# Interleaving three small layers with the gate products of the next column block, in a four-layer graph network on one core

## The chip, the core and the metric

The kernel runs on one core of a Trainium2 chip. The metric is the device time of one execution in microseconds (us). The core has a matrix engine (TensorE, "PE" in the profile; its weight loads are "PEld"), a vector engine (VectorE, "DVE"), an activation engine (ScalarE, "ACT"), GpSimd ("POOL") and the engine that issues transfers here (SyncE, "SP"). Each engine runs its own instructions strictly in the order of the program, and they wait for one another through semaphores. TensorE writes its results to eight banks of PSUM, `PS[0]` to `PS[7]`; ScalarE and VectorE carry them from there to SBUF.

## The reference

Four graph layers work one after the other on 1875 nodes with 256 features. The change lies in the second one, after its messages have been summed into `agg` per node. What follows there is, for each node on its own:

```python
gates = agg @ W_ih.T + b_ih + b_hh
i, f, g, o = jnp.split(gates, 4, axis=-1)
c = jax.nn.sigmoid(i) * jnp.tanh(g)
hn = jax.nn.sigmoid(o) * jnp.tanh(c)
x = jax.nn.relu(hn @ W1.T + b1)
x = jax.nn.relu(x @ W2.T + b2)
return x @ W3.T + b3
...
x = _layernorm(x + _L1_gnn_ref(...), axis=-1)
```

The gate `f` isn't used, so 3 x 256 gate features are computed: six pieces of 128. `W1` takes 256 features to 128, `W2` 128 to 128, `W3` 128 to 256.

## The kernel before

All engines' programs are written out by hand, with waits by hand; nothing plans or reorders them. The 1875 nodes are padded to 1920, which are `NC` = 5 column blocks of `CN` = 384 nodes. In the gate stage a block c goes through these steps:

- TensorE, `gates(c)`: six products (j = 0 to 5), each of two parts k, into `PS[0]` to `PS[5]` (L1796). A product j of block c waits until ScalarE has emptied the same bank of block c-1 (`gate_ev`). In the trace a float32 product of 384 columns shows as two matmul records, so one block's gates are 24 records.
- ScalarE, L748: six evacuations with Sigmoid or Tanh into the tile `GT`, j = 0 to 5. The first of block c waits for `hn_ready` of block c-1, since there is only one `GT`.
- VectorE, L1332: `CC` = the product of gates 0, 1 with 2, 3; it waits for evacuation 3 of the block. ScalarE, L750: tanh of `CC`. VectorE, L1337: `HN` = `CC` times gates 4, 5; this counts `hn_ready`.
- The three small layers: TensorE multiplies by W1 into `PS[6]` (L1813, waits for `hn_ready`), ScalarE applies Relu into `X1` (L757); TensorE multiplies by W2 into `PS[7]` (L1816), ScalarE applies Relu into `X2` (L759); TensorE adds the bias row and multiplies by W3 for three tiles of 128 nodes, into `PS[6]` and `PS[7]` (L1820, L1821). This is called x1, x2, x3 below.
- VectorE, L1349 and L1350: adds the result to `X` and counts `x3_add`; x1 of the next block waits for that. Only then does VectorE come to L1332 of the next block.

TensorE's order is: gates(0); 15 small products that count degrees (L1804); and then for each block c: gates(c+1), x1(c), x2(c), x3(c). ScalarE's order is, per block: six evacuations, tanh, X1, X2. In blocks 2 and 3 ScalarE also converts a piece of the adjacency counts between tanh and X1 (`early_cast`, L733, in a branch). In block 1 VectorE also splits four bias rows (L1221 to L1227) behind `HN`. In the last block VectorE normalises the first twelve node tiles between `HN` and the adds, with a square root from ScalarE (`ln_sqrt(5, ...)`, L671).

When x3 of the last block is done (`x3_mm`), SyncE loads six weights of the third layer (L477) over the place of the old ones, and TensorE's products of the third layer (`project`, L1831 and L1833) wait for them.

Of the kernel before, what the change touches and what calls it, by code (L numbers as in the profile page):

```python
# [29 lines left out]
ACT = mybir.ActivationFunctionType  # L30
# [6 lines left out]
NT = -(-N // P)  # L37
# [72 lines left out]
CN = 3 * P  # L110
NC = NP // CN
# [57 lines left out]
def build(nc, rec, x, xT, edge0, w0, a0l, a0r, cols, hrow, wrel, brow, wih, w1, w2, w3, b3, wp1, bp1, wl1, bl1, wr1, wp2, bp2, wl2, bl2, wr2,  # L169
          wt3, a3l, a3r, out):  # L170
    ctx = ExitStack()
    with ctx:
# [26 lines left out]
        BC = sb("bias_cols", [P, 32], F32)  # L199
# [13 lines left out]
        PS = [BANKS[:, 512 * i:512 * (i + 1)] for i in range(8)]  # L213

        def ar(off, *dims, dt=None):
            n = 1
            for d in dims:
                n *= d
            v = AR[:, off:off + n]
            if len(dims) == 2:  # L220
                v = v.rearrange("p (a b) -> p a b", b=dims[1])
            elif len(dims) == 3:
                v = v.rearrange("p (a b c) -> p a b c", b=dims[1], c=dims[2])
            return v
# [123 lines left out]
        GT = ar(A_B1, 6, CN)  # L348
        CC, HN, X1, X2 = ar(A_B1 + 6 * CN, 2, CN), ar(A_B1 + 8 * CN, 2, CN), ar(A_B1 + 10 * CN, CN), ar(A_B1 + 11 * CN, CN)
# [11 lines left out]
        s = {n: sem(n) for n in names}  # L361
# [210 lines left out]
        def _(act):  # L572
            a = nc.scalar
# [95 lines left out]
            def ln_sqrt(n, t0, t1):  # L669
                act.wait_ge(s["var_ready"], n)  # L670
                a.activation(RS[:, t0:t1], MV[:, t0:t1, 1], ACT.Sqrt).then_inc(s["std_ready"], 1)  # L671
# [64 lines left out]
            def early_cast(v, c):  # L736
                with act.If(large < 1):
                    cast2(v, c, False)
                with act.If(large >= 1):
                    cast2(v, c, True)  # L740

            funcs = (ACT.Sigmoid, ACT.Sigmoid, ACT.Tanh, ACT.Tanh, ACT.Sigmoid, ACT.Sigmoid)
            for c in range(NC):
                for j in range(6):
                    act.wait_ge(s["gate_mm"], 6 * c + j + 1)
                    if j == 0 and c:
                        act.wait_ge(s["hn_ready"], c)
                    a.activation(GT[:, j, :], PS[j][:, 0:CN], funcs[j], bias=BC[:, 20 + j:21 + j]).then_inc(s["gate_ev"], 1)  # L748
                act.wait_ge(s["c_ready"], c + 1)
                a.activation(CC, CC, ACT.Tanh).then_inc(s["tc_ready"], 1)  # L750
                if c in (2, 3):
                    act.wait_ge(s["bias_ready"], 2)
                    early_cast(0, c - 2)
                if c == NC - 1:
                    ln_sqrt(5, 0, NT - 3)
                act.wait_ge(s["x1_mm"], c + 1)
                a.activation(X1, PS[6][:, 0:CN], ACT.Relu, bias=BC[:, 18:19]).then_inc(s["x1_ev"], 1)  # L757
                act.wait_ge(s["x2_mm"], c + 1)
                a.activation(X2, PS[7][:, 0:CN], ACT.Relu, bias=BC[:, 19:20]).then_inc(s["x2_ev"], 1)  # L759
            ln_sqrt(6, NT - 3, NT)  # L760
            for q in range(4):
                xt_evac(1, q)
# [704 lines left out]
        def _(pe):  # L1467
# [95 lines left out]
            for i in range(4 * NT):  # L1563
                if i in between:
                    between[i]()
                t, c = i // 4, i % 4
# [147 lines left out]
            def transpose_x(n, q, src, ready, before):  # L1714
                pe.wait_ge(ready, before + q + 1)
                if n >= 2 and q >= 2:
                    xt_ready(n, q - 2)
                for k in range(2):
                    for j in range(min(4, NT - 4 * q)):
                        ins = tr(PS[xt_bank(n, q) + k][:, P * j:P * (j + 1)], src[:, 4 * q + j, P * k:P * (k + 1)], ident[:, :])  # L1720
                    ins.then_inc(s["xt_mm"], 1)
# [65 lines left out]
            pe.wait_ge(s["agg_evd"], 1)  # L1787
            pe.wait_ge(s["agg_eva"], 4)

            def gates(c):  # L1790

                for j in range(6):
                    if c:
                        pe.wait_ge(s["gate_ev"], 6 * c - 5 + j)
                    for k in range(2):
                        ins = mm(PS[j][:, 0:CN], WIH[:, k, P * j:P * (j + 1)], XT[:, k, CN * c:CN * (c + 1)],  # L1796
                                 start=(k == 0), stop=(k == 1))
                    ins.then_inc(s["gate_mm"], 1)

            gates(0)  # L1800
            pe.wait_ge(s["cnt_red"], 1)
            for t in range(NT):
                w = min(P, NW - P * t)
                ins = mm(PS[7][0:w, t:t + 1], CNTS[:, P * t:P * t + w], ones[:, 0:1], start=True, stop=True)  # L1804
            ins.then_inc(s["cnt_mm"], 1)
            for c in range(NC):
                if c + 1 < NC:
                    gates(c + 1)
                pe.wait_ge(s["hn_ready"], c + 1)
                if c:  # L1810
                    pe.wait_ge(s["x3_add"], c)
                for k in range(2):
                    ins = mm(PS[6][:, 0:CN], W1s[:, k, :], HN[:, k, :], start=(k == 0), stop=(k == 1))  # L1813
                ins.then_inc(s["x1_mm"], 1)
                pe.wait_ge(s["x1_ev"], c + 1)
                mm(PS[7][:, 0:CN], W2s, X1, start=True, stop=True).then_inc(s["x2_mm"], 1)  # L1816
                pe.wait_ge(s["x2_ev"], c + 1)
                for j in range(3):
                    o = PS[6 + j // 2][:, D * (j % 2):D * (j % 2 + 1)]
                    mm(o, ones16[0:3, :], BP[0:3, 2, :], start=True, stop=False)  # L1820
                    ins = mm(o, X2[:, P * j:P * (j + 1)], W3s, start=False, stop=True)  # L1821
                ins.then_inc(s["x3_mm"], 1)
            for q in range(4):
                transpose_x(1, q, X, s["ln_done"], 4)

# [111 lines left out]
```

## Time and profile before

| | |
|---|---|
| median of 3 runs | 1783.98 us (1782.76 to 1784.89) |
| the profiled execution: its own time | 1781.72 us |
| span of the profiled execution, first to last instruction | 1780.0 us |
| busy in the span: PE, DVE, ACT, POOL | 80%, 65%, 42%, 31% |
| mean granted TensorE clock (share of full speed) | 0.76 |
| gate stage: first gate product to the last small layer's end | 1364.52 to 1448.05 us |

Busy shares are averages over stages with different limits. The stage of the change is about 84 us of the span, and the granted clock in it is at either of two levels, 1.00 (2.4 GHz) or 0.50 (1.2 GHz).

### The profile page before, as it was taken

The page shows a single profiled execution, that of the slowest core. Times are in us where ns is not written, and L with a number is a line of the kernel's source. Part 1 is how long each engine was busy: PE and PEld are TensorE (multiplying, and loading weights), DVE is VectorE, ACT ScalarE, POOL GpSimd, SP SyncE. Part 2 cuts the span into 40 slices and gives each one's busy share as a digit, 9 for nine tenths or more (in the row PEclk, how much of TensorE's full clock was granted, in tenths as well). Part 3 has the DMA queues.
Part 4 walks back from the last instruction along what each step waited for, and adds up shares of the span by engine and source line. Part 5 has one row for each costly group of instructions (what it writes and reads, how often), then busy time and mean ns, then how long its engine had stood idle before and what let it go on. Part 6 is the DMA issues. An engine that isn't in the chain of part 4 may idle for free.

```text
span 1780.0 us, 21845 instructions
## 1 busy us (share of the span) xinstructions
PE 1422.1 (80%) x5158; PEld 758.0 (43%) x5158; DVE 1154.4 (65%) x2990; ACT 749.8 (42%) x1243; POOL 546.0 (31%) x517
## 2 busy tenths in 40 slices
PE   5897987777777777773499999798999989989840
PEld 2454643411111111112277777454445447758630
DVE  6323543399999999999989988751180443543727
ACT  1333443477777777772000000236774435416022
POOL 0103777777777777771000000000000000000023
PEclk9997555755555555555599999898999979999965
DMA  4534666655555555552098888000000010000023
GB/s 163 167 133 154 210 210 213 211 185 187 185 186 185 179 187 184 186 185 85 25 322 275 266 273 256 1 1 26 1 1 2 0 36 0 2 12 1 1 62 74
DMA packets 84507, 223.90 MB, mean 126 GB/s; under 512 B 18456, under 2 KB 27588, under 8 KB 83908
## 3 DMA queue, kind: packets, MB, share of 16 engines
q1 hardware_dynamic: 60452, 158.01, 25.4%
q0 software_dynamic: 23968, 64.77, 14.0%
q8 instruction: 51, 0.84, 0.2%
q14 instruction: 36, 0.29, 0.1%
HBM read 140.09 MB, written 82.63 MB: 125 GB/s over the span
## 4 chain that ended last, share of the span: by engine, by line
PE 43%; DVE 20%; issue 14%; POOL 6%; DMA 2%; ACT 2%; DVEq 2%; SPq 0%; POOLq 0%
PE bank L1776 14%; PE bank L1711 13%; POOL arena L557 6%; DVE arena L1095 4%; DVE arena L1096 3%; DVE adjacency L1102 3%; PE bank L1796 2%; DVE arena L1137 2%; PE bank L1833 2%; PE bank L1758 2%; PE bank L1733 2%; DMA arena<-feat_table,arena 1%; PE bank L1865 1%; DVEq L372 1%; PE bank L1862 1%
## 5 line engine op out<-in xcount | busy, mean ns | idle before, releaser
L557 POOL DMA_INDIRECT arena<-feat_table,arena x469 | 508.8, 1085 | 240.1 <-issue 227.9
L1650 PE MATMUL bank<-arena 128*128 128x480 f16 x586 | 337.0, 576 | 122.0 <-DVE arena L1096 116.0
L639 ACT ACTIVATE arena<-bank 128x480 uint16<-128x480 f32 x586 | 333.4, 572 | 118.1 <-PE bank L1650 111.6
L565 POOL DMA_INDIRECT arena<-al_table,edge_ends x15 | 14.8, 985 | 917.4 <-DMA al_table<-arena 913.2
L1102 DVE TENSOR_TENSOR adjacency<-adjacency,arena 128x480 uint16 x586 | 235.5, 402 | 9.9 <-DVE arena L1115 6.2
L1650 PEld LDWEIGHTS bank<-arena 128*128 128x128 f16 x586 | 61.0, 104 | 398.3 <-DVE arena L1096 312.0
L1711 PE MATMUL bank<-arena 128*128 x966 | 229.6, 392 | 0.9 <-issue 0.3
L1096 DVE TENSOR_SCALAR arena<-iota,arena 128x480 f16<-128x480 f16 x586 | 199.2, 340 | 0.0
L1711 PEld LDWEIGHTS bank<-arena 128*128 128x128 f32 x966 | 173.4, 190 | 57.3 <-issue 36.4
L1193 DVE TENSOR_TENSOR arena<-arena 128x1024 f32<-128x1024 f32 x118 | 140.1, 1214 | 16.4 <-DMA arena<-edge_rows 14.5
L1776 PE MATMUL bank<-arena 128*128 128x472 f16 x720 | 146.2, 367 | 3.9 <-ACT arena L713 3.9
L1095 DVE TENSOR_SCALAR arena<-iota,arena 128x128 f16<-128x128 f16 x586 | 145.9, 249 | 1.3 <-ACT adjacency L603 1.3
L713 ACT ACTIVATE arena<-adjacency 128x1888 f16<-128x1888 uint16 x30 | 109.0, 3638 | 34.9 <-PE bank L1776 34.9
L1570 PE MATMUL bank<-arena 128*128 128x512 f32 x240 | 108.8, 608 | 5.7 <-ACT arena L588 3.0
L1776 PE MATMUL bank<-count_chunks,message_halves 128*128 128x472 f32 x480 | 103.4, 377 | 2.1 <-DVE message_halves L1293 2.1
L1776 PEld LDWEIGHTS bank<-arena 128*128 128x128 bf16 x720 | 71.1, 99 | 79.3 <-ACT arena L713 4.7
L671 ACT ACT_TABLE_LOAD x2 | 2.6, 1283 | 240.0 <-DVE ln_mean_var L1239 240.0
L1776 PEld LDWEIGHTS bank<-count_chunks,message_halves 128*128 128x128 f32 x480 | 90.0, 188 | 15.5 <-issue 2.9
L1613 PE MATMUL bank<-arena 128*128 x588 | 75.7, 189 | 17.1 <-DVE arena L1052 11.3
L733 ACT ACTIVATE count_chunks<-adjacency 128x944 fp32r<-128x944 uint16 (+1 forms) x30 | 69.9, 2335 | 39.8 <-PE bank L1776 39.8
L1613 PEld LDWEIGHTS bank<-arena 128*128 128x128 f16 x588 | 60.1, 105 | 48.4 <-issue 35.0
L1200 DVE TENSOR_TENSOR arena<-iota,arena 128x1024 f32<-128x1024 f16 (+1 forms) x61 | 73.8, 1210 | 7.0 <-PE bank L1711 6.9
(294 smaller groups left out, 1598.0 us busy)
## 6 DMA issues: line engine op xcount, KB each, us to landing
arena<-edge_rows SPq DMA_DIRECT2D x117, 520.0 KB, 4.7
edge_rows<-arena SPq DMA_DIRECT2D x67, 520.0 KB, 2.9
edge_rows<-arena SPq DMA_DIRECT2D x67, 390.0 KB, 2.6
feat_table<-arena SPq DMA_DIRECT2D x60, 260.0 KB, 2.1
arena<-feat_table,arena POOLq DMA_INDIRECT x469
arena<-in_w SPq DMA_DIRECT2D x1, 2048.0 KB, 9.7
arena<-in_xT SPq DMA_DIRECT2D x1, 1920.0 KB, 18.0
arena<-in_x SPq DMA_DIRECT2D x1, 1792.0 KB
```

Source lines behind the costliest of these rows:

```text
L557: g.indirect_dma_start(out=PLACE[k][:, t - lo, :], out_offset=None, in_=feat_t, in_offset=bass.IndirectOffsetOnAxis(ap=IE[:, t:t + 1], axi ...
L639: a.activation(EV[st % AS].rearrange("p r k -> p (r k)"), PS[4 + st % 4][:, 0:R2 * KW], ACT.Copy)\
L713: a.activation(chunk(CH1, c % 2, wide), ADJ[:, r, :].rearrange("p (n s) -> p n s", s=SH)[:, :, sh], ACT.Copy).then_inc(s["chunk_ready"], 1)
L1095: v.tensor_scalar(OHS[st % AS], iota128[:, :], lo, None, ALU.is_equal)
L1096: v.tensor_scalar(OHK[st % AS], iota480[:, :], key, None, ALU.is_equal).then_inc(s["a_oh"], 1)
L1102: v.tensor_tensor(dst, dst, EV[st % AS], ALU.add).then_inc(s["a_add"], 1)
L1193: v.tensor_tensor(rows, rows, al, ALU.mult).then_inc(s["r_wgt"], 1)
L1570: ins = mm(PS[c][:, :], XT0[:, k, P * t:P * (t + 1)], W0[:, k, 512 * c:512 * (c + 1)], start=(k == 0), stop=(k == 1))
L1613: ins = mm(PS[4 + g % 2][:, 3 * H * k:3 * H * (k + 1)], KO[g % 3][:, lo:lo + P], ERW[:, bass.ds(offs[k], 3 * H)], start=True, stop=True)
L1650: mm(PS[4 + st % 4][:, 0:R2 * KW], OHS[st % AS], OHK[st % AS], start=True, stop=True).then_inc(s["a_mm"], 1)
L1711: mm(BANKS[:, bass.ds(out_at, D)], OHR[:, (st // RG) % ORING, P * (st % RG):P * (st % RG + 1)], FBf[:, bass.ds(places[st % RK] >> 12, D)], ...
L1776: ins = mm(PS[4 * fo + j][:, 0:CW], m[:, P * fo:P * (fo + 1)], ch[:, CW * j:CW * (j + 1)], start=(c == 0 and q == 0), stop=(c == n - 1 and ...
```

## The change

TensorE no longer computes all six gate products of block c+1 ahead of the small layers of block c. It computes three of them, then x1(c), the fourth, x2(c), the fifth, x3(c), the sixth. ScalarE's order follows, and two other pieces move on it: the conversions of blocks 2 and 3 come behind X2 in place of ahead of X1, and the square root of the last block is written ahead of the (there empty) gate evacuations. VectorE's and SyncE's programs are the same.

```diff
             funcs = (ACT.Sigmoid, ACT.Sigmoid, ACT.Tanh, ACT.Tanh, ACT.Sigmoid, ACT.Sigmoid)
+            def gate_out(c, j):
+
+                act.wait_ge(s["gate_mm"], 6 * c + j + 1)
+                if j == 0 and c:
+                    act.wait_ge(s["hn_ready"], c)
+                a.activation(GT[:, j, :], PS[j][:, 0:CN], funcs[j], bias=BC[:, 20 + j:21 + j]).then_inc(s["gate_ev"], 1)
+
+            for j in range(6):
+                gate_out(0, j)
             for c in range(NC):
-                for j in range(6):
-                    act.wait_ge(s["gate_mm"], 6 * c + j + 1)
-                    if j == 0 and c:
-                        act.wait_ge(s["hn_ready"], c)
-                    a.activation(GT[:, j, :], PS[j][:, 0:CN], funcs[j], bias=BC[:, 20 + j:21 + j]).then_inc(s["gate_ev"], 1)
                 act.wait_ge(s["c_ready"], c + 1)
                 a.activation(CC, CC, ACT.Tanh).then_inc(s["tc_ready"], 1)
+                if c == NC - 1:
+                    ln_sqrt(5, 0, NT - 3)
+                if c + 1 < NC:
+                    for j in range(3):
+                        gate_out(c + 1, j)
+                act.wait_ge(s["x1_mm"], c + 1)
+                a.activation(X1, PS[6][:, 0:CN], ACT.Relu, bias=BC[:, 18:19]).then_inc(s["x1_ev"], 1)
+                if c + 1 < NC:
+                    gate_out(c + 1, 3)
+                act.wait_ge(s["x2_mm"], c + 1)
+                a.activation(X2, PS[7][:, 0:CN], ACT.Relu, bias=BC[:, 19:20]).then_inc(s["x2_ev"], 1)
                 if c in (2, 3):
                     act.wait_ge(s["bias_ready"], 2)
                     early_cast(0, c - 2)
-                if c == NC - 1:
-                    ln_sqrt(5, 0, NT - 3)
-                act.wait_ge(s["x1_mm"], c + 1)
-                a.activation(X1, PS[6][:, 0:CN], ACT.Relu, bias=BC[:, 18:19]).then_inc(s["x1_ev"], 1)
-                act.wait_ge(s["x2_mm"], c + 1)
-                a.activation(X2, PS[7][:, 0:CN], ACT.Relu, bias=BC[:, 19:20]).then_inc(s["x2_ev"], 1)
+                if c + 1 < NC:
+                    for j in (4, 5):
+                        gate_out(c + 1, j)
...
-            def gates(c):
-
-                for j in range(6):
+            def gates(c, js):
+
+                for j in js:
+                    if c == NC:
+                        break
...
-            gates(0)
+            gates(0, range(6))
...
             for c in range(NC):
-                if c + 1 < NC:
-                    gates(c + 1)
+                gates(c + 1, range(3))
                 pe.wait_ge(s["hn_ready"], c + 1)
...
                 ins.then_inc(s["x1_mm"], 1)
+                gates(c + 1, (3,))
                 pe.wait_ge(s["x1_ev"], c + 1)
                 mm(PS[7][:, 0:CN], W2s, X1, start=True, stop=True).then_inc(s["x2_mm"], 1)
+                gates(c + 1, (4,))
                 pe.wait_ge(s["x2_ev"], c + 1)
...
                 ins.then_inc(s["x3_mm"], 1)
+                gates(c + 1, (5,))
```

On TensorE, from the degree counts on, block 0 stood like this before (one row may stand for several instructions, `x12` for the six gate products of two parts each; L1796 is a gate product, L1813 x1, L1816 x2, L1820 and L1821 x3):

```order
3655 L1804 MATMUL bank<-ones,arena 96x1
3656 L1796 MATMUL bank<-arena 128x384 x12
3657 L1813 MATMUL bank<-arena 128x384 x2
3658 L1816 MATMUL bank<-arena 128x384
3659 L1820 MATMUL bank<-arena,ones 128x256
3660 L1821 MATMUL bank<-arena 128x256
```

The same place in the changed program, where a gate product is L1810, x1 is L1826, x2 L1830, and x3 L1835 and L1836:

```order
3655 L1818 MATMUL bank<-ones,arena 96x1
3656 L1810 MATMUL bank<-arena 128x384 x6
3657 L1826 MATMUL bank<-arena 128x384 x2
3658 L1810 MATMUL bank<-arena 128x384 x2
3659 L1830 MATMUL bank<-arena 128x384
3660 L1810 MATMUL bank<-arena 128x384 x2
3661 L1835 MATMUL bank<-arena,ones 128x256
3662 L1836 MATMUL bank<-arena 128x256
3663 L1835 MATMUL bank<-arena,ones 128x256
3664 L1836 MATMUL bank<-arena 128x256
3665 L1835 MATMUL bank<-arena,ones 128x256
3666 L1836 MATMUL bank<-arena 128x256
```

So three gate products now stand ahead of x1, one between x1 and x2, and one between x2 and x3. At the end of the small layers of block 3 the changed TensorE program goes on like this:

```order
3698 L1835 MATMUL bank<-arena,ones 128x256
3699 L1836 MATMUL bank<-arena 128x256
3700 L1810 MATMUL bank<-arena 128x384 x2
3701 L1826 MATMUL bank<-arena 128x384 x2
3702 L1830 MATMUL bank<-arena 128x384
```

The sixth gate product of block 4 now stands between x3(3) and x1(4), where nothing stood. On ScalarE, before, the tanh of block 2 (L750), its conversion (L733, in the taken branch of two), its two Relus (L757, L759) and the gates of block 3 (L748) stood like this:

```order
492 L750 ACTIVATE arena<-arena 128x768
493 L737 COMPARE_AND_BRANCH
494 L733 ACTIVATE count_chunks<-adjacency 128x1888
495 L737 UNCONDITIONAL_BRANCH
496 L739 COMPARE_AND_BRANCH
497 L733 ACTIVATE arena<-adjacency 128x1888
498 L739 UNCONDITIONAL_BRANCH
499 L757 ACTIVATE arena<-bank,bias_cols 128x384
500 L759 ACTIVATE arena<-bank,bias_cols 128x384
501 L748 ACTIVATE arena<-bank,bias_cols 128x384 x6
```

The same block in the changed program, where tanh is L754 and the Relus are L761 and L765:

```order
496 L754 ACTIVATE arena<-arena 128x768
497 L748 ACTIVATE arena<-bank,bias_cols 128x384 x3
498 L761 ACTIVATE arena<-bank,bias_cols 128x384
499 L748 ACTIVATE arena<-bank,bias_cols 128x384
500 L765 ACTIVATE arena<-bank,bias_cols 128x384
501 L737 COMPARE_AND_BRANCH
502 L733 ACTIVATE count_chunks<-adjacency 128x1888
503 L737 UNCONDITIONAL_BRANCH
504 L739 COMPARE_AND_BRANCH
507 L748 ACTIVATE arena<-bank,bias_cols 128x384 x2
```

The conversion moved from ahead of both Relus to between the second Relu and the last two gate evacuations of block 3. No load of an activation table was added or moved among these rows.

## Rows read from the trace of the kernel before

**Rows 1.** Chain that ended last, blocks 0 and 1: start us, us, what.
```profile
1378.43 7.85 PE bank L1796 x24
1386.28 1.30 PE bank L1813 x4
...
1392.42 7.74 PE bank L1796 x24
1400.16 1.30 PE bank L1813 x4
...
1401.48 0.59 ACT arena L757
...
1402.12 0.93 PE bank L1816 x2
...
1403.07 0.59 ACT arena L759
...
1403.70 0.28 PE bank L1820
...
1406.29 7.74 PE bank L1796 x24
```

**Rows 2.** The same chain, from x1 of block 3 to the third layer.
```profile
1427.90 1.30 PE bank L1813 x4
...
1434.08 0.02 DVEq L1347
...
1437.95 2.60 PE bank L1813 x4
...
1448.05 0.41 SPq L477
...
1455.41 0.39 PE bank L1831
```

**Rows 3.** Timeline of DVE: start us, us, line, what, [idle before <-releaser].
```profile
1380.96 0.96 DVE L1337 TENSOR_TENSOR arena<-arena 128x768 f32<-128x768 f32 x1 [0.91 <-ACT arena L750]
...
1395.25 0.96 DVE L1337 TENSOR_TENSOR arena<-arena 128x768 f32<-128x768 f32 x1 [0.91 <-ACT arena L750]
...
1402.98 1.27 DVE L1227 SCALAR_TENSOR_TENSOR arena<-arena,ident 3x1024 bf16<-3x1024 bf16 x1
```

**Rows 4.** Timeline of ACT, block 2, and two conversions in a row later.
```profile
1408.32 0.84 ACT L750 ACTIVATE arena<-arena 128x768 f32<-128x768 f32 x1 [1.84 <-DVE arena L1332]
1409.07 3.63 ACT L733 ACTIVATE count_chunks<-adjacency 128x1888 fp32r<-128x1888 uint16 x1
1415.36 0.58 ACT L757 ACTIVATE arena<-bank,bias_cols 128x384 f32<-128x384 f32 x1 [2.65 <-PE bank L1813]
...
1532.24 7.14 ACT L733 ACTIVATE count_chunks<-adjacency 128x1888 fp32r<-128x1888 uint16 x2
```

**Rows 5.** Windows: busy by engine, then PEclk (granted clock), DMA share, GB/s.
```profile
1378.30:1434.00 55.70, 50.32 (x158) 27.01 (x157) 20.72 (x33) 26.22 (x38) 0.00 (x0) 1.00 0.00 0
1438.00:1448.00 10.00, 8.65 (x16) 3.62 (x17) 6.16 (x29) 1.58 (x4) 0.00 (x0) 0.52 0.00 0
1532.90:1533.80 0.90, 0.90 (x4) 0.67 (x4) 0.00 (x0) 0.90 (x1) 0.00 (x0) 1.00 0.00 0
1533.90:1537.30 3.40, 3.40 (x9) 2.59 (x9) 0.88 (x2) 3.40 (x2) 0.00 (x0) 0.50 0.00 0
1651.80:1653.20 1.40, 1.40 (x6) 0.90 (x7) 0.00 (x0) 0.00 (x0) 0.00 (x0) 1.00 0.06 12
1653.40:1656.80 3.40, 3.40 (x9) 2.05 (x7) 1.33 (x4) 0.00 (x0) 0.00 (x0) 0.50 0.00 0
```

**Rows 6.** Timeline of PE, the two places of rows 5 that follow an idle time.
```profile
1532.89 1.13 PE L1862 MATMUL bank<-arena 128*128 128x256 f32 x4 [2.48 <-DVE arena L1315]
...
1651.78 1.13 PE L1862 MATMUL bank<-arena 128*128 128x256 f32 x4 [2.48 <-DVE arena L1315]
```

## The prediction, made before the changed kernel ran

> **What bounds the kernel now.** I read the chain of work that ended last first, in order of time, because only what stands on it can shorten the run. From the end of the degree counts to the last gate product this chain is TensorE, broken by two short ScalarE pieces per block [rows 1]. One block is 13.87 us (1392.42 to 1406.29): 7.74 us of gate products, 1.30 us of x1, then a Relu of 0.59 us on ScalarE, x2, another Relu of 0.59 us, and x3 from 1403.70 to 1406.29, 2.59 us. During both Relus TensorE stands still: x1 starts at 1400.16 and is 1.30 long, but x2 starts only at 1402.12, 0.66 us after x1's end; x2 starts at 1402.12 and x3 at 1403.70, 1.58 us for two matmul records. At the steady rate of 7.74 / 24 = 0.3225 us per record, two take 0.65 us, so 0.93 us of that is waiting for the drain and the Relu.
>
> Then I followed the chain to where the stage hands over [rows 2]. x3(3) ends at 1434.08; x1(4) starts at 1437.95, 3.87 us later, because VectorE's adds, CC, tanh on ScalarE and HN stand between and no TensorE work is left. x1(4) to x3(4) then take 10.10 us (1437.95 to 1448.05). The same layers of block 3 take 6.18 us (1427.90 to 1434.08). The windows say why: the granted clock is 1.00 from 1378.3 to 1434.0 and 0.52 from 1438 to 1448 [rows 5], nearly all of it at the lower of the two levels. At 1448.05 SyncE starts the next layer's weights, and that layer's first product waits for them until 1455.41. What comes behind is tied to that moment, so whatever the stage saves, the span should save.
>
> **The change part by part.** No arithmetic is added or removed; the costs are all order.
>
> *Start.* Before, x1(0) comes behind all of gates(1), 7.85 us from 1378.43, and starts at 1386.28 [rows 1]. Now three of six products stand ahead of it: 7.85 / 2 = 3.92 us, so x1(0) could start at 1382.35. It needs HN(0), which ends at 1380.96 + 0.96 = 1381.92 [rows 3], 0.4 us earlier. Gain 3.9 us. The cover is thin: if HN(0) were later by more than 0.4 us, the rest would be lost one for one.
>
> *Steady blocks.* TensorE's own work per block is 7.74 + 1.30 + 0.65 + 2.59 = 12.28 us. The fourth gate product (two parts, 7.74 / 6 = 1.29 us) stands where TensorE waited 0.66 us for X1. With x1 starting at time 0, x1 ends at 1.30, the gate product at 2.59, and X1 is ready at 1402.12 - 1400.16 = 1.96: no wait. x2 runs from 2.59, the fifth gate product to 4.53; X2 is ready 1.58 us after x2's start, at 4.17: no wait. x3 ends at 7.12, the sixth product at 8.41, three products of the next block at 12.28. What could be late there is HN. Before, x1(4) came 3.87 us behind x3(3) through exactly this sequence [rows 2], so HN is ready at 7.12 + 3.87 = 10.99, 1.3 us before x1 wants it. A block is then 12.28 in place of 13.87: three periods between x1(0) and x1(3) give 3 x 1.59 = 4.8 us.
>
> *ScalarE's order in blocks 2 and 3.* The conversion (3.63 us) was covered by 2.65 us of idle time behind it [rows 4]. Now the last two gate evacuations queue behind it, and behind these tanh, HN and x1. X2 ends at about 4.1, the conversion at 7.8, the fifth evacuation (0.58) at 8.3; the sixth can't start before its product at 8.41, and ends at 9.0. Tanh is due when CC is there: it started 2.03 us after x3's end before (1408.32 against 1406.29 [rows 1, 4]), so at 9.15. The conversion fits with about nothing over. The two branches around it are the unknown: from below nothing, since two conversions in a row took 7.14 us, less than 2 x 3.63 [rows 4]; from above 2.65 us, the idle time that could hide them before. I take nothing, as the row of two conversions is the nearest. Block 2 has the 1.3 us of HN's slack as well.
>
> *VectorE in block 1.* The bias split begins behind HN and ended 8.04 us after it (1396.21 to 1404.25 [rows 3]). HN(1) now ends 1.3 us before x1(1), so the split ends at 6.7 after it, before x3(1) at 7.12. Nothing is lost.
>
> *End.* x1(4) needs HN(4). From x1(3) it comes at 10.99, where it was 10.05 (1427.90 to 1437.95): three gate products of 1.29 us now stand between the small layers, and only the Relu waits pay for two of them. Loss 0.9 us.
>
> *The clock.* TensorE's idle time ahead of x1(4) shrinks from 3.9 us to 10.99 - 8.41 = 2.6 us. Whether the clock falls again decides up to 10.10 - 6.18 = 3.9 us. The nearest rows are two idle times of 2.48 us later in the kernel [rows 6]. After both, dense products began at 1.00 and the clock then stood at 0.50: still full 0.9 us after the first restart and 1.4 us after the second, low from 1.0 and 1.6 us on [rows 5, 6]. So I expect the fall here too, but with some 0.9 us of x1(4) at full speed, work that takes twice as long at half: 1.30 against 2.60 us for x1 [rows 2]. I take 0.9 us of gain, with bounds of 0 and 3.9.
>
> The Trainium skill ("TensorE: Matmul & The Clock Gate", section "Why this matters for your kernels") advises to keep idle gaps between bursts of matmuls short, and the gap from which it warns of a slow restart is longer than the wait forecast here. By that page x1(4) to x3(4) would run at full speed and the gain would be 7.8 + 3.9 = 11.7 us. The two rows after 2.48 us of idle time speak against it, and the measurement decides.
>
> **Sum.** 3.9 + 4.8 - 0.9 = 7.8 us, and 0.9 for the clock: 8.7 us. The profiled execution took 1781.72 us, so its like would take 1773.0. The median of the runs shown is 2.3 us above that execution, so I forecast 1783.98 - 8.7 = 1775.3 us.
>
> **The rivals.** *The clock stays up.* Gain 11.7 us, 1772.3 us. For it: a shorter idle time than before, and 1.00 throughout the blocks with their waits. Against it: rows 5 and 6.
>
> *HN comes late in the blocks.* The branches hold ScalarE, or the evacuations pile up more than I have laid out. With 2.65 us in both blocks, block 2 loses 2.65 - 1.3 and block 3 all of it: 4.0 us, gain 4.7, 1779.3 us. For it: three pieces of work end within 0.2 us of each other in my layout. Against: the two conversions back to back.
>
> *The gain is taken back at the weights.* If the third layer waited for something other than the weights, say VectorE's normalisation, the stage would be shorter and the span not: 1784 us. Against it: the chain goes through the SyncE issue at 1448.05 and the landing before 1455.41, with no wait of another kind between.
>
> *Slower: the clock falls inside a block.* With products and waits interleaved otherwise, TensorE might drop to half speed among the gates. Rows 2 price it: x1 takes 2.60 for 1.30, so a block at half speed costs some 12 us more, and one such block outweighs the 8.7 us: 1783.98 - 8.7 + 12 = 1787.3 us. It decides from the first whole block. Against it: 1.00 from 1378.3 to 1434.0 with 0.66 and 0.93 us of waits per block, and the change shortens these.
>
> **How the numbers follow.** Chances: forecast 0.62, clock stays up 0.12, HN late 0.13, no gain 0.08, slower 0.05. The four times of before spread over 3.1 us (1781.72 to 1784.89), so each case carries some 1.5 us either way. The range from 1771.0 to 1779.5 holds the first two cases and about half of the third, some 8 in 10. A change under 0.2% (3.6 us) can't be told from none. Faster needs less than 1780.4 us: the first two cases and most of the third, 0.86. Same takes the fourth and the rest of the third, 0.09; slower 0.05.
>
> **What the changed profile would show.** Between the sixth evacuation of block 0 and x1(4), TensorE without idle time; x1 of successive blocks 12.3 us apart; x1(0) some 3.9 us behind the end of the counts; no wait of the gate products for evacuations. The idle time ahead of x1(4) would be 2.6 us, with granted clock falling within x1(4) or just behind it. I am wrong if x1 of some block waits for HN, if in blocks 2 and 3 ScalarE's fifth evacuation starts much later than the end of the conversion, or if x1(4) to x3(4) take about 6 us.

## The result, and the profile after

The changed kernel takes 1772.19 us (median of 4 runs, 1768.48 to 1773.56), the kernel before 1783.37 us in the runs beside it. The ratio is 0.9941, with a 95% interval of 0.9914 to 0.9967: faster by 0.6%, and the whole interval lies below 1. In two more sets of runs (e10 and e12 below) the same kernel stood at 0.9941 (0.9922 to 0.9960) and 0.9931 (0.9907 to 0.9956). The forecast was 1775.3 us.

The profiled execution took 1768.48 us, with a span of 1766.8 us. That is 13.2 us shorter than the profiled span before; 2.8 us of it lie ahead of the gate stage (first gate product at 1361.70 us, before at 1364.52), where nothing was changed. So stages are compared below from the first gate product on.

The chain that ended last, from the end of the degree counts to x1 of block 1, answers to [rows 1] (start us, us, what; gate products are now L1810, x1 L1826, x2 L1830, x3 L1835 and L1836):

```profile
1375.54 3.98 PE bank L1810 x12
1379.52 1.29 PE bank L1826 x4
1380.81 1.29 PE bank L1810 x4
1382.10 0.65 PE bank L1830 x2
1382.75 1.29 PE bank L1810 x4
1384.04 0.21 PE bank L1835
...
1386.56 5.16 PE bank L1810 x16
1391.72 1.29 PE bank L1826 x4
```

No ScalarE piece and no waiting is left in it: the chain is TensorE from end to end. x1(1) starts 12.20 us after x1(0); it was 13.87 us. x2 costs 0.65 us on the chain, where it cost 0.93. Between x1 and x2 and between x2 and x3 stands a gate product of 1.29 us, as laid out.

The end of the stage on the same chain answers to [rows 2] (L1344 is CC, L754 tanh, L1349 HN, L671 the square root, L761 the Relu X1, L477 the weights, L1847 the third layer's first product):

```profile
1423.14 1.12 PE bank L1810 x4
1424.26 0.88 DVE arena L1344
...
1425.17 0.85 ACT arena L754
...
1426.04 0.96 DVE arena L1349
1427.00 1.00 DVE ln_stats L1244 x3
...
1429.17 0.21 ACT ln_rstd L671
1429.38 0.48 ACT arena L761
...
1435.67 0.41 SPq L477
...
1443.43 0.28 PE bank L1847
```

One piece of it was in no part of the prediction: the chain doesn't go through x1(4), but through VectorE's statistics and the square root, behind which X1 stands on ScalarE. TensorE's timeline shows what that does (in brackets the idle time ahead and what ended it):

```profile
1427.05 1.56 PE L1826 MATMUL bank<-arena 128*128 128x384 f32 x4 [2.63 <-DVE arena L1349]
1429.90 0.91 PE L1830 MATMUL bank<-arena 128*128 128x384 f32 x2 [1.29 <-ACT arena L761]
1431.49 0.28 PE L1835 MATMUL bank<-arena,ones 3*128 3x256 bf16 x1 [0.67 <-ACT arena L765]
```

The idle time ahead of x1(4) is 2.63 us (forecast 2.6; before 3.9). Ahead of x2(4) it is 1.29 us in place of 0.67: with x1 at full speed, its Relu now has to wait for the square root. Before, x1(4) at half speed ended later than the root (root done at 1440.28 us, X1 from 1440.58), so the root held up nothing:

```profile
1437.95 2.59 PE L1813 MATMUL bank<-arena 128*128 128x384 f32 x4 [3.92 <-DVE arena L1337]
1441.22 1.65 PE L1816 MATMUL bank<-arena 128*128 128x384 f32 x2 [0.67 <-ACT arena L757]
```

ScalarE in block 2, where the conversion was moved, answers to [rows 4] (L748 gate evacuations, L765 the Relu X2, L733 the conversion):

```profile
1407.17 0.58 ACT L765 ACTIVATE arena<-bank,bias_cols 128x384 f32<-128x384 f32 x1
1407.65 3.61 ACT L733 ACTIVATE count_chunks<-adjacency 128x1888 fp32r<-128x1888 uint16 x1
1411.17 0.57 ACT L748 ACTIVATE arena<-bank,bias_cols 128x384 f32<-128x384 f32 x1
1412.27 0.58 ACT L748 ACTIVATE arena<-bank,bias_cols 128x384 f32<-128x384 f32 x1 [0.54 <-PE bank L1810]
1412.97 0.84 ACT L754 ACTIVATE arena<-arena 128x768 f32<-128x768 f32 x1
```

The branches cost nothing that shows: the fifth evacuation starts as the conversion ends, and ScalarE then waits 0.54 us for the sixth product. The layout had left 0.1 us there.

The granted clock by windows (busy by engine, then PEclk) answers to [rows 5]:

```profile
1375.40:1427.00 51.60, 49.03 (x158) 27.38 (x157) 23.56 (x38) 30.01 (x40) 0.00 (x0) 1.00 0.00 0
1427.05:1431.90 4.85, 2.88 (x8) 1.27 (x9) 4.47 (x24) 1.52 (x4) 0.00 (x0) 1.00 0.00 0
1432.00:1435.70 3.70, 3.70 (x10) 1.69 (x9) 1.66 (x7) 0.00 (x0) 0.00 (x0) 0.50 0.00 0
1443.40:1462.60 19.20, 19.14 (x75) 11.53 (x75) 5.95 (x14) 5.38 (x14) 0.00 (x0) 1.00 0.00 1
```

The clock still falls in the last small layers, but 4.9 us after x1(4)'s start and not within x1. The last row is new: the first products of the third layer run at full speed. Before, they did not:

```profile
1455.40:1462.20 6.80, 6.79 (x15) 3.82 (x15) 0.85 (x2) 0.77 (x2) 0.00 (x0) 0.50 0.01 2
```

All runs by stage, in us from their profiles: A from the first gate product to the start of x1(4); B from there to the start of the third layer's weights; C from that to the third layer's first product; D from that to the start of the product of its fifteenth and last node tile. "Idle" is TensorE's idle time ahead of x1(4). Each row is one profiled execution.

| run | A | idle | B | C | D | sum |
|---|---|---|---|---|---|---|
| before | 73.4 | 3.92 | 10.1 | 7.4 | 20.9 | 111.8 |
| before again (e8) | 73.4 | 3.92 | 10.2 | 7.6 | 20.7 | 111.9 |
| changed | 65.4 | 2.63 | 8.6 | 7.8 | 17.8 | 99.5 |
| changed again (e10) | 65.6 | 2.63 | 8.4 | 7.3 | 17.8 | 99.1 |
| changed, third (e12) | 65.6 | 2.62 | 8.4 | 7.5 | 17.8 | 99.3 |
| e1, TensorE's order only | 64.4 | 2.63 | 9.7 | 7.4 | 17.8 | 99.2 |
| e2, idle time filled | 65.3 | 0 | 8.7 | 7.4 | 17.8 | 99.1 |
| e3, square root behind X1 | 65.4 | 2.62 | 8.1 | 7.7 | 17.8 | 99.1 |
| e4, conversions twice | 72.5 | 5.79 | 10.4 | 8.0 | 20.9 | 111.7 |
| e5, filled, root behind X2 | 64.4 | 0 | 7.7 | 8.3 | 22.0 | 102.3 |
| e6, CC first | 64.3 | 1.72 | 6.8 | 7.6 | 23.1 | 101.9 |
| e11, CC first again | 64.5 | 1.72 | 6.8 | 8.0 | 19.9 | 99.2 |
| e9, CC first, root early | 64.5 | 1.72 | 7.1 | 7.9 | 19.9 | 99.3 |
| e7, one gap empty | 69.1 | 2.63 | 9.7 | 8.0 | 19.4 | 106.2 |

In e1 and e5 the clock rose sooner in the first six gate products (mean granted clock 0.62 in their first 3.6 and 3.1 us; in the changed kernel 0.50 in the first 4.0). They took 9.67 us in place of about 10.65; A is 1.0 us shorter there for that reason.

### The profile page after: what moved, and what is told of

It is laid out like the page before. It is cut to its first block, busy times and chain, and to the rows that moved or that the text cites. A ratio compares the mean times of both kernels' runs of the same rounds, so it can differ in the third digit from the quotient of the medians.

```text
span 1766.8 us, 21845 instructions
## 1 busy us (share of the span) xinstructions
PE 1416.2 (80%) x5158; PEld 757.8 (43%) x5158; DVE 1154.6 (65%) x2990; ACT 750.8 (42%) x1243; POOL 544.5 (31%) x517
## 3 DMA queue, kind: packets, MB, share of 16 engines
q1 hardware_dynamic: 60452, 158.01, 25.6%
## 4 chain that ended last, share of the span: by engine, by line
PE 53%; DVE 21%; issue 10%; POOL 5%; ACT 4%; DMA 3%; DVEq 2%; SPq 0%; POOLq 0%; ACTq 0%
PE bank L1788 14%; PE bank L1723 13%; PE bank L1582 6%; POOL arena L557 5%; DVE arena L1107 4%; ACT arena L639 3%; DVE arena L1108 3%; PE bank L1662 3%; DVE adjacency L1114 3%; PE bank L1810 2%; DVE arena L1149 2%; PE bank L1849 2%; PE bank L1770 2%; PE bank L1745 2%; DMA arena<-feat_table,arena 1%
## 5 line engine op out<-in xcount | busy, mean ns | idle before, releaser
L1114 DVE TENSOR_TENSOR adjacency<-adjacency,arena 128x480 uint16 x586 | 251.8, 430 | 10.4 <-DVE arena L1127 6.2
L1108 DVE TENSOR_SCALAR arena<-iota,arena 128x480 f16<-128x480 f16 x586 | 216.0, 369 | 0.0
L1107 DVE TENSOR_SCALAR arena<-iota,arena 128x128 f16<-128x128 f16 x586 | 163.1, 278 | 0.4 <-ACT adjacency L603 0.4
L733 ACT ACTIVATE count_chunks<-adjacency 128x944 fp32r<-128x944 uint16 (+1 forms) x30 | 69.9, 2334 | 39.7 <-PE bank L1788 39.7
```

The costliest lines, as they stand in the source:

```text
L1107: v.tensor_scalar(OHS[st % AS], iota128[:, :], lo, None, ALU.is_equal)
L1108: v.tensor_scalar(OHK[st % AS], iota480[:, :], key, None, ALU.is_equal).then_inc(s["a_oh"], 1)
L1114: v.tensor_tensor(dst, dst, EV[st % AS], ALU.add).then_inc(s["a_add"], 1)
```

## The experiments

**e1: TensorE's order alone.** ScalarE's program was put back to its old order; TensorE's stayed as changed.

```diff
             for c in range(NC):
+                for j in range(6):
+                    gate_out(c, j)
                 act.wait_ge(s["c_ready"], c + 1)
...
+                if c in (2, 3):
+                    act.wait_ge(s["bias_ready"], 2)
+                    early_cast(0, c - 2)
...
-                    for j in range(3):
-                        gate_out(c + 1, j)
```

> TensorE's new order with ScalarE's old one (six evacuations, tanh, the conversion, both Relus, per block). Theory A, the gain comes from TensorE's order alone: X1 can start 1.3 us after x1's start and the conversion before it ends about then; the six evacuations behind X2 take 6 x 0.49 us and the sixth still waits for its product, so the stage from the first gate product to the start of the third layer's weights is within 0.5 us of the changed kernel's 73.97 us. Theory B, ScalarE's order is needed: evacuations pile up behind X2, gate products wait for banks or x1 waits for HN, at least 1 us per block, and the stage is 78 us or more.

Measured: 1770.18 us, ratio 0.9935 (0.9911 to 0.9959); A + B is 74.1 us, as theory A has it, but in part by luck: A is 1.0 us shorter for the quicker first products (above), and B is 1.1 us longer since the clock fell sooner in it. What carries the reading are the distances between x1(0) and x1(3), 12.19 to 12.20 us as in the changed kernel, and the idle times. TensorE never waits between the first gate product and x1(4), and waits as long ahead of it as with the new order:

```profile
1427.77 1.62 PE L1818 MATMUL bank<-arena 128*128 128x384 f32 x4 [2.63 <-DVE arena L1341]
```

ScalarE, with all six evacuations behind X2, still has to wait for the sixth product (block 3):

```profile
1412.98 0.58 ACT L748 ACTIVATE arena<-bank,bias_cols 128x384 f32<-128x384 f32 x1 [2.16 <-PE bank L1802]
```

Theory A holds. ScalarE's new order, half of the diff, is worth nothing that shows.

**e2: the idle time ahead of x1(4) filled.** Two products whose results nobody uses:

```diff
                 gates(c + 1, range(3))
+                if c == NC - 1:
+                    for j in range(2):
+                        pe.wait_ge(s["gate_ev"], 6 * c + j + 1)
+                        for k in range(2):
+                            mm(PS[j][:, 0:CN], WIH[:, k, P * j:P * (j + 1)], XT[:, k, CN * c:CN * (c + 1)],
+                               start=(k == 0), stop=(k == 1))
```

> Two spare gate products (1.29 us each, results not used) stand in TensorE's idle time ahead of x1 of the last block. Theory A, the clock falls there because TensorE stands idle for 2.6 us: it now stays at full speed through the last small layers, which take 6.8 us from x1's start to the start of the weights (6.2 us as in the other blocks and 0.65 us for the square root ahead of X1), in place of 8.62 us. Theory B, the clock falls for another reason: 8.6 to 10.1 us, and x1 of the last block starts at the same time.

Measured: 1771.26 us, ratio 0.9938 (0.9917 to 0.9960). B is 8.7 us, as in the changed kernel. The idle time was gone (the row of x1(4) has none in brackets), and the clock fell all the same, 4.9 us after x1(4)'s start at 1429.57:

```profile
1429.57 1.56 PE L1832 MATMUL bank<-arena 128*128 128x384 f32 x4
```

The windows from there on:

```profile
1429.50:1434.40 4.90, 2.88 (x9) 1.25 (x9) 4.52 (x25) 1.59 (x4) 0.00 (x0) 1.00 0.00 0
1434.50:1438.20 3.70, 3.70 (x10) 1.67 (x9) 1.66 (x6) 0.00 (x0) 0.00 (x0) 0.50 0.00 0
```

Theory B: the wait of 2.6 us isn't needed for the fall. What remained ahead of it were 1.29 us behind the square root and 0.67 us at X2.

**e3: the square root behind X1.**

```diff
-                if c == NC - 1:
-                    ln_sqrt(5, 0, NT - 3)
...
                 a.activation(X1, PS[6][:, 0:CN], ACT.Relu, bias=BC[:, 18:19]).then_inc(s["x1_ev"], 1)
+                if c == NC - 1:
+                    ln_sqrt(5, 0, NT - 3)
```

> The square root of the last block's normalisation stands behind X1 on ScalarE in place of ahead of it. Theory A, X1 waited 0.65 us for it: X1 starts within 0.1 us of x1's end, and x1 to the start of the weights is 0.65 us shorter at the same clock behaviour (8.0 us in place of 8.62 us where the clock falls at the same place). Theory B, the normalisation then ends last and delays the third layer: the start of the weights comes earlier, but the wait for them or for what follows grows by as much.

Measured: 1770.10 us, ratio 0.9931 (0.9905 to 0.9957). The wait ahead of x2(4) is 0.67 us again, but X2 now stands behind the table load of 1.28 us and the root, and x3(4) waits 1.08 us in place of 0.67. B is 8.1 us: 0.5 us shorter than in the first profile of the changed kernel, 0.3 shorter than in the other two. The direction is theory A's, but 0.41 us came back as a wait for X2, which the expectation had not seen. The third layer gained nothing: B and C together are 15.9 us, in the changed kernel 15.7 to 16.4.

**e4: each conversion twice.**

```diff
                 if c in (2, 3):
                     act.wait_ge(s["bias_ready"], 2)
+                    early_cast(0, c - 2, True)
                     early_cast(0, c - 2)
```

> The conversions of blocks 2 and 3 run twice each (the second writes the same values again), 3.65 us more on ScalarE in each. Theory A, HN has 1.3 us of slack per block and the conversion some 0.6 us until tanh: x1(3) comes 3.7 - 0.6 - 1.3 = 1.8 us late and x1(4) another 3.7 - 0.6 = 3.1 us, so that the stage is about 4.9 us longer than the changed kernel's 73.97 us. Theory B, ScalarE has idle time for all of it: no difference. Theory C, none of it is hidden: 7.3 us longer.

Measured: 1781.71 us, ratio 0.9996 (0.9979 to 1.0013): the whole gain is gone. x1(3) and x1(4) wait for HN:

```profile
1422.11 2.73 PE L1832 MATMUL bank<-arena 128*128 128x384 f32 x4 [1.97 <-DVE arena L1355]
1438.19 2.29 PE L1832 MATMUL bank<-arena 128*128 128x384 f32 x3 [5.79 <-DVE arena L1355]
```

The waits are close to theory A's: 1.97 us (expected 1.8) and 5.79 - 2.63 = 3.16 us (expected 3.1), though each second conversion added some 4.1 us and not 3.65: a semaphore of its own now stands between the two, and ScalarE waited 0.44 us at it. The stage grew by 8.9 us, though, and not 4.9. After the first wait TensorE worked 3.3 us at half speed within block 3, and the last small layers took 10.4 us. So the waits cost more than their length in this run:

```profile
1422.40:1425.70 3.30, 3.30 (x6) 1.71 (x6) 0.65 (x2) 1.85 (x4) 0.00 (x0) 0.50 0.00 0
```

Another 3.1 us came back in D (20.9 in place of 17.8), where the third layer began at half speed again.

**e5: filled, and the square root behind X2.** e2's edit, with `ln_sqrt(5, ...)` moved behind X2.

> The two spare gate products ahead of x1 of the last block as in the run before, and the square root behind X2, so that nothing but the two Relus holds TensorE in the last small layers. Theory A, what lowers the clock there is idle time of any origin, and the 1.29 us behind the square root were enough by themselves: now only 0.67 us at each Relu are left, as in the blocks of the kernel before, where the clock stayed at 1.00, and x1 to the start of the weights takes 6.2 us. Theory B, the clock falls at this place whatever the idle time: 7.5 us or more. What it costs behind: the normalisation ends some 1.5 us later, and the third layer may wait up to 1 us longer behind the weights.

Measured: 1770.22 us, ratio 0.9932 (0.9913 to 0.9952). Theory A fails: with no wait over 0.67 us from x1(4) to x3(4), and none ahead of x1(4), the clock still fell, 4.7 us after x1(4)'s start at 1428.23, and the third layer's first products ran at half speed again:

```profile
1428.23 1.56 PE L1832 MATMUL bank<-arena 128*128 128x384 f32 x4
1430.46 0.91 PE L1836 MATMUL bank<-arena 128*128 128x384 f32 x2 [0.67 <-ACT arena L759]
1432.05 0.28 PE L1841 MATMUL bank<-arena,ones 3*128 3x256 bf16 x1 [0.67 <-ACT arena L763]
```

The windows:

```profile
1428.20:1432.90 4.70, 3.32 (x10) 1.38 (x10) 2.05 (x16) 2.05 (x3) 0.00 (x0) 1.00 0.00 0
1433.00:1435.90 2.90, 2.90 (x7) 1.54 (x7) 2.31 (x8) 0.51 (x2) 0.00 (x0) 0.50 0.00 0
1444.20:1453.30 9.10, 9.08 (x20) 5.09 (x20) 1.71 (x4) 1.15 (x3) 0.00 (x0) 0.50 0.01 3
```

B is 7.7 us, but C and D together are 30.3 us, in the changed kernel 25.1 to 25.6 us.

**e6 and e11: CC of the next block first.** VectorE's order, with ScalarE's tanh ahead of the sixth evacuation and the second conversion behind the last block; the square root as in e3.

```diff
+                if c + 1 < NC:
+                    dve.wait_ge(s["hn_ready"], c + 1)
+                    gated(c + 1)
                 dve.wait_ge(s["x3_mm"], c + 1)
...
+                    gate_out(c + 1, 4)
+                    gate_tanh(c + 1)
+                    gate_out(c + 1, 5)
```

Here `gated(c)` is the wait and the product of L1343 and L1344 of the changed kernel.

> VectorE multiplies CC of the next block ahead of the adds of x3, ScalarE applies its tanh ahead of the sixth evacuation, the second conversion moves behind the last block, and the square root stands between X1 and X2. If HN of the last block is bound by the chain adds, CC, tanh, HN, it is now bound by the sixth evacuation and HN: x1 of the last block comes 8.4 + 0.6 + 1.0 = 10.0 us after x1(3) in place of 10.9, TensorE's idle time ahead of it is 1.7 us in place of 2.63, and the periods of the blocks before stay at 12.2 us, since they are bound by TensorE. Rival: the sixth evacuation already set the end, and x1 of the last block moves by less than 0.3 us.

Measured: 1768.95 us, ratio 0.9927 (0.9908 to 0.9945). The idle time ahead of x1(4) is 1.72 us, as expected, and this time the clock held through the small layers; it fell behind them, and the third layer began at half speed:

```profile
1426.60 1.56 PE L1838 MATMUL bank<-arena 128*128 128x384 f32 x4 [1.72 <-DVE arena L1358]
```

The windows:

```profile
1426.60:1433.40 6.80, 5.04 (x17) 2.43 (x18) 5.05 (x26) 2.54 (x4) 0.00 (x0) 1.00 0.00 1
1433.40:1439.10 5.70, 2.63 (x25) 2.39 (x22) 5.56 (x18) 1.66 (x4) 0.00 (x0) 1.00 0.77 247
1441.00:1452.70 11.70, 11.70 (x27) 6.40 (x26) 2.25 (x5) 4.92 (x5) 0.00 (x0) 0.50 0.01 2
```

The stage is 2.8 us shorter than the changed kernel's, and D is 5.3 us longer. Between the stage and the third layer TensorE has its transposes and waits for VectorE's normalisation, which the late square root holds up (VectorE stands idle 1.65 us for it, in e9 0.28):

```profile
1439.57 1.54 PE L1744 MATMUL bank<-ident,arena 128*128 128x128 f32 x6 [3.54 <-DVE arena L1262]
```

The same kernel once more, on one chip with the changed one:

> The version with CC ahead of the adds and the square root between X1 and X2 once more, timed on one chip with the changed kernel. Theory A, its gate stage is 2.8 us shorter, and the clock's fall behind it takes most of that back: within 2 us of the changed kernel, with the third layer's first products at half speed. Theory B, the low clock there was chance: they run at full speed this time, and it is 3 us or more faster than the changed kernel.

Measured: 1772.08 us, ratio 0.9942 (0.9919 to 0.9965), the changed kernel beside it 1771.20 us. Theory A: the stage is 2.7 us shorter again, the third layer began at half speed again (D 19.9 us; in e6 23.1), and the times can't be told apart.

**e7: one gap left empty.** ScalarE's evacuations follow (four ahead of X1, none between X1 and X2); TensorE's part of the edit:

```diff
-                gates(c + 1, range(3))
+                gates(c + 1, range(4))
...
-                gates(c + 1, (3,))
```

> Four gate products ahead of x1 and none between x1 and x2; the rest as in the changed kernel. Theory A, a product between two small layers gains exactly the Relu wait that it fills: 0.66 us in each of four blocks, so TensorE idles 0.67 us ahead of x2 again, the periods are 12.85 us, and x1 of the last block comes 2.6 us later than in the changed kernel. Theory B, the gain comes from elsewhere (the earlier start of x1(0), or HN's cover): no difference, or the whole 8 us back.

Measured: 1773.18 us, ratio 0.9945 (0.9923 to 0.9967). Block 1 from x1 to the product behind x2, and x2 of block 2:

```profile
1393.96 1.46 PE L1824 MATMUL bank<-arena 128*128 128x384 f32 x4
1396.09 0.91 PE L1827 MATMUL bank<-arena 128*128 128x384 f32 x2 [0.67 <-ACT arena L761]
1396.84 1.45 PE L1808 MATMUL bank<-arena 128*128 128x384 f32 x4
...
1409.22 0.91 PE L1827 MATMUL bank<-arena 128*128 128x384 f32 x2 [0.67 <-ACT arena L761]
```

The wait is back, and the period is 13.13 us (1396.09 to 1409.22): 0.93 us over the changed kernel's 12.20, not 0.66. x1(4) comes 69.1 - 65.4 = 3.7 us later, four times 0.93. Theory A, with a larger size: an idle time of 0.67 us by the profile costs TensorE 0.93 us, 0.26 us more than the idle time. The rows say where these lie: with nothing behind it x1 takes its full 1.46 us, where the next product follows after 1.29 us in the changed kernel, and from x2 to the next product it is 0.75 us (1396.09 to 1396.84), in the changed kernel 0.65; 0.16 + 0.67 + 0.10 = 0.93. The 3.7 us can be read in the stage alone: the run's ratio can't be told from the changed kernel's, whose three sets lie between 0.9931 and 0.9941.

**e8: the kernel before again; e10 and e12: the changed one again.**

> The kernel before once more, for a second profile. Theory A, whether the clock falls again at the first products of the third layer (7 us at half speed in the profile of before, none in that of the changed kernel, 3.1 us of the span) is by chance of the execution: this profile may show it or not, and the gate stage takes 83.5 us but for the moment at which the clock rises and falls. Theory B, it belongs to the order before: it shows again, and the 3.1 us are part of the change's gain.

> The changed kernel once more, for a second profile and times on the same chip as the version with CC first. Theory A, order sets the stage and chance sets the clock behind it: the gate stage takes 74 us again within 0.5 us plus what the clock does in the last small layers (8.6 to 10.1 us), and the first products of the third layer may be at half speed this time. Theory B, the clock's rise ahead of the third layer belongs to the new order: full speed at its first products again.

> The changed kernel, for the comparison on the same chip. Its stage takes 74.0 us again and the third layer's first products run at full speed, as in its two profiles before; its time is 10 to 12 us under the kernel before.

e8 took 1783.35 us (one run), e10 1770.11 us and e12 1771.20 us. A, B and D repeat to 0.2 us, C to 0.5 us (table); the stage of the changed kernel, A + B, is 74.0 us all three times. Windows of the first products of the third layer in e8, and then of those in e12:

```profile
1457.85:1464.20 6.35, 6.35 (x14) 3.81 (x15) 0.85 (x2) 0.77 (x2) 0.00 (x0) 0.50 0.01 3
```

```profile
1448.20:1467.00 18.80, 18.74 (x74) 11.52 (x75) 5.94 (x14) 5.39 (x14) 0.00 (x0) 1.00 0.00 1
```

Half speed in both profiles of before, full speed in all three of the changed kernel, and D is 17.8 us in e1, e2 and e3 too. That speaks for theory B of both expectations. Chance isn't excluded, though: the runs of the kernel before spread from 1774.78 to 1788.03 us, and no profile was taken of one of its short ones. What would tie the clock there to the order isn't shown either.

**e9: CC first, square root ahead of X1 again.**

> As the kernel with CC ahead of the adds, but with the square root ahead of X1 again, as in the changed kernel. Theory A, the late square root delayed the normalisation and so TensorE's last six transposes (idle 3.54 us ahead of them), and that long wait let the clock fall at the third layer's first products: now the normalisation ends about 1.3 us earlier, the idle time ahead of the transposes is about 2.5 us, x1 of the last block to the start of the weights stays near 6.8 us, and the run is 0 to 3 us faster than with the late square root. Theory B, the weights alone set the third layer's start: same start, and any difference is the moment at which the clock falls.

Measured: 1774.03 us, ratio 0.9951 (0.9932 to 0.9970); the changed kernel beside it took 1770.11 us. The idle time ahead of the last transposes is 2.52 us, as theory A has it, but the third layer starts at half speed all the same and D is 19.9 us. The weights set its start (7.9 us after their issue):

```profile
1446.54 0.39 PE L1859 MATMUL bank<-arena,ones 3*128 3x256 bf16 x1 [1.66 <-DMA arena<-in_wr]
```

Theory B. No version here beats the changed kernel clearly: e5, e6, e9 and e11, which shortened the stage by 1.9 to 2.8 us, gave it back in C and D.

## Why the prediction was right

**Steady blocks.** Right in mechanism: both Relu waits are covered, HN is never late (in blocks 1 to 3 it ends 1.1 to 1.2 us ahead of x1, forecast 1.3), and blocks are bound by TensorE's own work. The period was forecast at 12.28 us and measured at 12.20. Both gaps together are worth 13.87 - 12.20 = 1.67 us, where the sum had 1.59. Its split was off: it priced the gap behind x1 at 0.66 us, and e7 shows 0.93.

**Start and end.** x1(0) starts 3.98 us behind the counts, forecast 3.92, and HN(0) was in time by 0.3 us (it ended at 1379.03, and x1(0) starts at 1379.36 in the timeline; forecast 0.4). The wait ahead of x1(4) is 2.63 us (2.6). From the first gate product x1(4) comes 73.4 - 65.4 = 8.0 us earlier (7.8 by the other profiles), forecast 7.8. e1 shows that TensorE's order alone does this.

**ScalarE's order.** The conversion was forecast to fit with nothing over, and it fits with 0.54 us. e4 shows that the cover is real and small: another 4.1 us on ScalarE in each of two blocks makes the stage 8.9 us longer.

**The clock.** The term was 0.9 us in B, with the fall at about 1 us into x1(4). B shrank by 10.1 - 8.6 = 1.5 us, as the fall came at 4.9 us, even though the square root, which had no term, took 0.62 us of that back. That the clock would fall in B was right; the moment was not, and that the term comes out near is luck. The reason given, the wait of 2.6 us, is not the whole one: e2 and e5 have no such wait and the clock falls; e6 has 1.72 us, 0.67 us and 1.08 us of waits and it holds in B. The Trainium skill ("TensorE: Matmul & The Clock Gate", section "Why this matters for your kernels") advises to keep idle gaps between bursts short. e5 kept those from x1(4) to x3(4) at 0.67 us and the clock fell, so short gaps were not enough here. What decides the moment stays open.

**What the sum left out.** D: 20.9 - 17.8 = 3.1 us, the third layer's first products at full speed. No term stood for them, although half speed there was in the trace of before; the prediction took what comes behind the weights as tied to their start alone. That is most of the difference between the forecast gain of 8.7 us and the 12.3 us by which the profile's sum over A to D shrank (111.8 to 99.5). The medians differ by 11.2 us, in the other two sets by 10.8 and 12.0. The rest of the kernel varies: the first gate product came between 1361.7 and 1367.2 us in the 14 profiles, with nothing changed ahead of it.

**The rivals.** None came: the clock did not stay up through B, HN is not late, the weights' wait did not grow by the gain (C 7.4 to 7.8 us), and no block fell to half speed except in e4, where waits were added. The rival of the clock staying up had 1772.3 us, nearly the 1772.19 measured, but that is a coincidence: it needed 3.9 us in B, and B gave 1.5; the rest came from D.

## What to carry to other kernels

Where a chain of small products waits for its evacuations, put independent products of the next block into the gaps, one per gap, and check that whatever the next block needs is ready by the time they are done: the sum, in matmul records from the trace, was good to 0.1 us per block. Such a filled gap can be worth more than the idle time that the profile names (here 0.93 us for 0.67 us). Follow the granted clock beyond the stage that changes: here 3.1 of some 12 us came from products 8 us behind it, and further gains in the stage were lost there.

## What the hardware showed that was not expected

The clock fell in the last small layers 4.7 to 5.1 us after their start in the changed kernel and in e2, e3 and e5, whether TensorE had stood idle 2.6 us ahead of them or not at all, and 1.1 and 1.4 us after it in e7 and e1. In e6, e9 and e11 it held there and was then at half speed for the third layer's first products. In these profiles half speed came in one of the two places or in both, never in none. Once, in e4, a wait of 1.97 us ahead of a dense block was followed by 3.3 us at half speed within it.
